# Keys of a delta-rule memory fed to the tensor engine as 32x32 blocks, without block-diagonal copies

## The reference, cut to what matters

```
S = S * exp(g)                       # decay, per head and mode
kv = k @ S                           # read the memory with the key
dv = (v - kv) * beta                 # what the memory got wrong
S = S + outer(k, dv)                 # correct it
o += mode_weight * (q @ S)           # summed over the 8 modes
```

## Time and profile before

| | us |
|---|---|
| median of 3 runs | 8003.09 |
| lowest and highest run | 7991.04 to 8010.95 |
| the profiled execution's own time | 7953.85 |
| its span, first to last instruction | 7951.7 |
| mean granted clock of the tensor engine, share of full | 0.82 |

### The profile page before, as it was taken

How to read it: one execution, slowest core, us unless ns; L and a number is a source line. 1 busy time by engine, 2 the same in 40 slices (tenths; PEclk the granted TensorE clock), 3 DMA queues, 4 the chain that set the end, 5 groups by cost and what they waited for, 6 DMA issues and landing times. The chain is left out here.

```text
span 7951.7 us, 264166 instructions
## 1 busy us (share of the span) xinstructions
PE 5413.0 (68%) x111401; PEld 4716.2 (59%) x111401; DVE 5656.2 (71%) x11457; ACT 3642.4 (46%) x7127; POOL 1241.2 (16%) x740
## 2 busy tenths in 40 slices
PE   0676667666776677666766667666676667766994
PEld 0666656556666666566665666556666556655663
DVE  6777777777777777777777787777777777776003
ACT  0454445544544455544544455544454445554220
POOL 0111111111111111111111111111111111111003
PEclk9787888777877787887878888888887888887997
DMA  2000000000000000000000000000000000000223
GB/s 75 2 6 6 6 6 4 4 6 6 6 6 6 6 4 6 4 6 6 6 6 6 6 4 6 4 6 6 6 6 6 6 6 4 6 4 9 87 75 95
DMA packets 60431, 104.35 MB, mean 13 GB/s; under 512 B 11296, under 2 KB 48736, under 8 KB 58080
## 3 DMA queue, kind: packets, MB, share of 16 engines
q1 hardware_dynamic: 50784, 61.66, 2.4%
q0 software_dynamic: 8448, 25.18, 1.0%
HBM read 53.25 MB, written 33.55 MB: 11 GB/s over the span
## 5 line engine op out<-in xcount | busy, mean ns | idle before, releaser
L765 ACT ACTIVATE state<-state,gc_end 128x128 f32<-128x128 f32 x2048 | 650.1, 389 | 1432.4 <-PE bank L569 1430.9
L563 PE MATMUL bank<-rhs,tt 32*32 32x64 f32 x16384 | 407.0, 248 | 874.7 <-DVE rhs L1256 874.6
L563 PEld LDWEIGHTS bank<-rhs,tt 32*32 32x32 f32 x16384 | 316.3, 125 | 961.5 <-issue 944.4
L582 PE MATMUL last_two<-dvs,kte 128*64 128x64 f32 x16384 | 716.4, 254 | 150.3 <-DVE dvs L1263 150.3
L634 PE MATMUL bank<-tmp,turn_mat 32*32 32x128 f32 x24576 | 745.3, 279 | 48.4 <-issue 34.1
L545 PE MATMUL bank<-state,ke 128*64 128x64 f32 x16384 | 647.3, 246 | 167.3 <-issue 128.8
L582 PEld LDWEIGHTS last_two<-dvs,kte 128*64 128x64 f32 x16384 | 655.1, 167 | 164.9 <-DVE dvs L1263 157.2
L634 PEld LDWEIGHTS bank<-tmp,turn_mat 32*32 32x32 f32 x24576 | 709.8, 110 | 71.5 <-issue 65.4
L800 ACT ACTIVATE ke<-kq 32x512 f32<-32x512 f32 x1024 | 641.9, 627 | 238.1 <-DVE kq L1191 226.0
L545 PEld LDWEIGHTS bank<-state,ke 128*64 128x64 f32 x16384 | 605.2, 159 | 238.9 <-issue 184.2
L1239 DVE TENSOR_TENSOR last_two<-last_two,prod 128x31 f32<-128x31 f32 (+15 forms) x1984 | 692.5, 349 | 68.1
(11 more groups left out here) (236 smaller groups left out, 9821.8 us busy)
## 6 DMA issues: line engine op xcount, KB each, us to landing
w_sb<-in_L_ffn_W_dram SPq DMA_DIRECT2D x16, 1024.0 KB, 9.6
expert_rows<-ke SPq DMA_DIRECT2D x1, 8192.0 KB, 21.0
xrows<-expert_rows SPq DMA_DIRECT2D x16, 512.0 KB, 8.7
expert_outputs<-yrow POOLq DMA_DIRECT2D x16, 512.0 KB, 3.4
xt<-_attn_hidden_states_dram SPq DMA_DIRECT2D x32, 128.0 KB, 2.4
xr<-_attn_hidden_states_dram SPq DMA_DIRECT2D x32, 128.0 KB, 3.0
x_after_attention<-xr SPq DMA_DIRECT2D x32, 128.0 KB, 1.7
xo<-x_after_attention SPq DMA_DIRECT2D x32, 128.0 KB, 3.6
```

The costliest lines, as they stand in the source:

```text
L563: pe.matmul(bank_mem[g][s, q % 4 * DK:q % 4 * DK + DK], tt[s, c, q, :], rhs[s, q, :], start=True, stop=True)
L582: mm = pe.matmul(bank_upd[g][s, (q % 4) * P + r * DK:(q % 4) * P + r * DK + DK], kte[:, r, q, s], dvs[:, q, :], start=True, stop=True)
L765: ins = act.activation(state[:, vh * HQ + q], state[:, vh * HQ + q], ACT.Copy, scale=gc_end[:, vh, q, c:c + 1])
```

## The change

Gram, read and update take the keys directly from `kq` and `kt`, one 32x32 matmul per mode (`MODES`, four slices of 32 partitions) in place of one 128x64 matmul per side, so each of the three groups has 128 records in place of 64. `ke`, `kte`, the ACT functions that fill them, their calls and their semaphores go. Since the copies no longer carry the keys over to the next half, `kq` and `kt` get a second buffer, chosen by `hh`. Ahead of each group of 32x32 matmuls PE gets one semaphore increment (`pe_held`), as the corrections have it already. `gram` now waits for `k_rotated`, the update for `kt_ready`. The scratch areas of the set-up move from `ke` to `kq`, and one clearing of `kte` on POOL goes.

```diff
-        kt = sb("kt", [P, 2, HQ, P])
+        kt = sb("kt", [P, 2, 2, HQ, P])
-        kq = sb("kq", [P, 2, HQ, 2, P])
-        ke = sb("ke", [P, NC, 2, HQ, P])
-        kte = sb("kte", [P, 2, HQ, P])
+        kq = sb("kq", [P, 2, 2, HQ, 2, P])
...
-            def gram(u, c):
+            def gram(u, hh, c):
...
-                pe.wait_ge(sem("ke_ready"), 4 * u + c + 1)
+                pe.wait_ge(sem("k_rotated"), since("k_rotated", u + 1))
...
+                    pe.sem_inc(sem("pe_held"), 1)
                     for q in range(HQ):
                         for r in range(2):
-                            for s in SIDES:
-                                mm = pe.matmul(b[s, q * 2 * C:(q + 1) * 2 * C], ke[:, c, r, q, s],
-                                               kq[:, r, q, :, c * C:c * C + C], start=(r == 0), stop=(r == 1))
+                            for s in MODES:
+                                mm = pe.matmul(b[s, q * 2 * C:(q + 1) * 2 * C], kq[s, hh, r, q, 0, c * C:c * C + C],
+                                               kq[s, hh, r, q, :, c * C:c * C + C], start=(r == 0), stop=(r == 1))
...
+                    pe.sem_inc(sem("pe_held"), 1)
                     for q in range(4 * g, 4 * g + 4):
                         for r in range(2):
-                            for s in SIDES:
-                                mm = pe.matmul(bank_mem[g][s, q % 4 * DK:q % 4 * DK + DK], ke[:, c, r, q, s],
-                                               state[:, hh * HQ + q, r, :], start=(r == 0), stop=(r == 1))
+                            for s in MODES:
+                                mm = pe.matmul(bank_mem[g][s, q % 4 * DK:q % 4 * DK + DK], kq[s, hh, r, q, 0, c * C:c * C + C],
+                                               state[s, hh * HQ + q, r, :], start=(r == 0), stop=(r == 1))
...
-                    pe.wait_ge(sem("kte_ready"), vc + 1)
+                    pe.wait_ge(sem("kt_ready"), v + 1)
+                    pe.sem_inc(sem("pe_held"), 1)
...
-                            for s in SIDES:
+                            for s in MODES:
                                 mm = pe.matmul(bank_upd[g][s, (q % 4) * P + r * DK:(q % 4) * P + r * DK + DK],
-                                               kte[:, r, q, s], dvs[:, q, :], start=True, stop=True)
+                                               kt[s, hh, r, q, c * C:c * C + C], dvs[s, q, :], start=True, stop=True)
...
-            def expand_kte(v, c):
...
-            def expand_ke(v, c):
...
-            def turn_keys(u, first):
-                if not first:
-                    dve.wait_ge(sem("kte_ready"), 4 * u)
-                ln(dve.transpose(kt[:, 0], kq[:, 0, :, 0, :]))
-                vec(dve.transpose(kt[:, 1], kq[:, 1, :, 0, :]), "kt_ready", u + 1)
+            def turn_keys(u, hh):
+                ln(dve.transpose(kt[:, hh, 0], kq[:, hh, 0, :, 0, :]))
+                vec(dve.transpose(kt[:, hh, 1], kq[:, hh, 1, :, 0, :]), "kt_ready", u + 1)
```

More of the change, by code:

```diff
@@ L273, in build @@
         xg = tmp[:, 3, 0:4 * P].rearrange("p (c m j) -> p c m j", c=NC, m=4)
+        scratch = kq[:].rearrange("p a r q s t -> p (a r q s t)")
         at = cos_t[:].rearrange("p q t -> p (q t)").rearrange("p (c q i) -> p c q i", c=NC, q=HQ)
@@ L279, in build @@
         sq = rhs[:].rearrange("p q v -> p (q v)").rearrange("p (h t) -> p h t", h=HH)
-        wmod_sb = ke[:].rearrange("p a b c d -> p (a b c d)")[:, 0:KC * 6 * D].rearrange("p (k n) -> p k n", k=KC)
-        onehot = ke[:].rearrange("p a b c d -> p (a b c d)")[:, 0:Q * NEXP].rearrange("p (q e) -> p q e", q=Q)
-        picked = ke[:].rearrange("p a b c d -> p (a b c d)")[:, Q * NEXP:2 * Q * NEXP].rearrange("p (q e) -> p q e", q=Q)
+        wmod_sb = scratch[:, 0:KC * 6 * D].rearrange("p (k n) -> p k n", k=KC)
+        onehot = scratch[:, 0:Q * NEXP].rearrange("p (q e) -> p q e", q=Q)
+        picked = scratch[:, Q * NEXP:2 * Q * NEXP].rearrange("p (q e) -> p q e", q=Q)
         turn_tab = qg[:].rearrange("p r q t -> p (r q t)")[:, 0:7 * NEXP].rearrange("p (k e) -> p k e", k=7)
@@ L373, in _ @@
             sp.wait_ge(sem("setup_done"), 1)
-            zero_row = ke[:].rearrange("p c r q j -> p (c r q j)")[:, 0:2048]
+            zero_row = scratch[:, 0:2048]
             sp.dma_start(slots_dram[0:E * CAP, :].rearrange("(a p g) d -> p a (g d)", p=P, g=8),
@@ L671, in half @@
                     corrections(v, vh, 3)
-                gram(u, 0)
+                gram(u, hh, 0)
                 rows(4 + hh)
                 if not first:
[L675 to L678, removed]
+                    update_and_outputs(v, vh, 3)
+                gram(u, hh, 1)
+                gram(u, hh, 2)
+                gram(u, hh, 3)
                 if hh == 0 and not first:
@@ L834, in half @@
                 for s in range(2):
-                    if s == 0 and not first:
-                        act.wait_ge(sem("upd_full1"), since("upd_full1", 4 * v + 2))
-                        expand_kte(v, 2)
                     take(lambda b: act.activation(raw[:, s].rearrange("p h t -> p (h t)"), b[:, :], ACT.Copy))
@@ L845, in half @@
                     take_dv(v, vh, 2)
-                act.wait_ge(sem("k_rotated"), since("k_rotated", u + 1))
-                expand_ke(u, 0)
-                if not first:
-                    act.wait_ge(sem("upd_full1"), since("upd_full1", 4 * v + 3))
-                    expand_kte(v, 3)
-                expand_ke(u, 1)
                 if not first:
                     take_dv(v, vh, 3)
-                expand_ke(u, 2)
-                expand_ke(u, 3)
                 clear_inverse(v, first)
@@ L881, in half @@
                     gap(n - 1)
-                if not first:
-                    act.wait_ge(sem("upd_full1"), since("upd_full1", 4 * v + 4))
-                act.wait_ge(sem("kt_ready"), u + 1)
-                expand_kte(u, 0)
             def route(t):
@@ L1052, in _ @@
             lp(dve.tensor_copy(pos[:], pos0))
-            lp(dve.memset(ke[:], 0.0))
+            lp(dve.memset(scratch, 0.0))
             lp(dve.memset(count[:], 0.0))
@@ L1190, in rotate_keys @@
                     else:
-                        vec(dve.tensor_tensor(kq[:, 1, :, 0, :], tm[0], tm[1], ALU.subtract), "k_rotated", u + 1)
+                        vec(dve.tensor_tensor(kq[:, hh, 1, :, 0, :], tm[0], tm[1], ALU.subtract), "k_rotated", u + 1)
             def beta_decays(u, hh):
@@ L1200, in beta_decays, with queries_for_memories @@
                                            dec[:, s4].rearrange("p q c i -> p (q c i)"), ALU.mult))
-            def turn_keys(u, first):
-                if not first:
-                    dve.wait_ge(sem("kte_ready"), 4 * u)
-                ln(dve.transpose(kt[:, 0], kq[:, 0, :, 0, :]))
-                vec(dve.transpose(kt[:, 1], kq[:, 1, :, 0, :]), "kt_ready", u + 1)
-            def queries_for_memories(u):
+            def turn_keys(u, hh):
+                ln(dve.transpose(kt[:, hh, 0], kq[:, hh, 0, :, 0, :]))
+                vec(dve.transpose(kt[:, hh, 1], kq[:, hh, 1, :, 0, :]), "kt_ready", u + 1)
+            def queries_for_memories(u, hh):
                 dve.wait_ge(sem("q_rotated"), since("q_rotated", u + 1))
@@ L1360, in half @@
                 memories(right_sides, 3)
-                turn_keys(u, first)
+                turn_keys(u, hh)
                 memories(decayed_corrections, 3)
                 chunk_systems(u, 0)
-                queries_for_memories(u)
+                queries_for_memories(u, hh)
                 memories(update_memories, 3)
@@ L1430, in _ @@
             pool.wait_ge(sem("setup_done"), 1)
-            vec(pool.memset(kte[:], 0.0), "clear_step", 1)
-            vec(pool.memset(ones[:], 1.0), "clear_step", 2)
+            vec(pool.memset(ones[:], 1.0), "clear_step", 1)
             for i in range(4):
```

36 lines of the change are left out of this document (16 added, 20 removed).

## The result

The changed kernel takes 8245.22 us (median of 4 runs, 8238.91 to 8247.92) against 8006.41 for the kernel before in the same comparison: ratio 1.0301, 95% interval 1.0283 to 1.0318, so 239 us slower. The forecast said slower, 8090 us, and at most 8230: the right side and the right mechanism, but a third of the size, and the result lies above its range. The profiled execution took 8247.92 us, close to the median; that of before was 0.6% quicker than its runs.

The account below looks back on a forecast made before the run. No engine full: each half is a chain between DVE, PE and ACT. Per half -0.5 + 0.6 + 1.15 = +1.25 us; 63 halves +79, with the after-loop part +88: 7953.85 becomes 8042, scaled to 8090 us; range 7950 to 8230.

Parts of the forecast that it names:

- ACT's relief: Chunk 1's second update no longer waits for ACT's key copy: 0.5 us gained a half, -31 us over 63 halves.
- Work and shape: On PE, 128 small records take 1.8 to 2.3 us against 2.09 before; shape changes add 0.4 and 0.1 us.
- The supply's price: Instruction fetching for PE: one packet, some 125 records, per 3.54 us, so 128 records take 3.6 us when starved.
- Rival 1: Instruction supply keeps up on PE, only the -31 us stand: 7972 us, range 7945 to 8003; chance 0.30.
- part (c): After the loop: 128 more records in each of three chunks, 3 us each, 9 us in all.
- Where it hits: Places of instruction shortage: chunk 1 +0.6 us a half, update 3 to last Gram +1.15, after the loop 9 in all.
- chunks up to Gram 0: Chunk 0's shape changes and chunk 1's earlier update gain 0.6 us a half; chunk 1's instruction shortage costs 0.6.
- Gram 0 itself: One change of matmul shape ahead of the first Gram product: +0.1 us a half.
- from update 3 to root or residual: 528 records in a row outrun the instruction packets: +1.5 us with `hh` 0, +0.8 with `hh` 1, mean +1.15.
- The tail of halves with `hh` 1: From update 3, the last Gram ends 13.1 us later, at 3059.6 against 3058.86 before: +0.8 us.
- Rival 2, the clock: Starved PE is granted the lower clock, a group costs 3.61 us instead of 2.09: about 8280 us; chance 0.12.

## Why the prediction was right and wrong

**ACT's relief: right.** Forecast -31 us, bounds 0 to -57; measured -22 without the added records, and PE's wait for the copy is gone.

**Work and shape: right.** 127 records took 2.00 us, 15.7 ns each, against 14.2 to 18.1 forecast; with half as many records the shape cost nothing that can be measured.

By the floor of about 25 ns in the Trainium skill, "TensorE: Matmul & The Clock Gate", section "Wait — 56ns, not 53.3ns?", 128 would have taken 3.2 us, as an estimate; the timelines contradict it.

**The supply's price: nearly right.** 125 records in 3.54 us were taken; it is 128 in 3.75. Some 1350 packets were forecast, 1342 came. Rival 1 would have had no gaps of "issue". After the loop, part (c), 9 us were forecast; from the first read there to `project_out` the two timelines differ by 10.8.

The Trainium skill, "Runtime: NRT & Kernel Launch", section "Instruction fetch mechanics", has the block of 256 instructions, and 128 pairs a packet agree; that the crossing of a block is mostly hidden, the gaps of 0.9 to 1.8 us at each block contradict.

**"Where it hits": the step that failed.** It let the shortage be felt once in the chunks, in the chain of three Grams, and nowhere else. Against the table of the result, in us a half: chunks up to Gram 0, forecast 0 net, measured 0.71; Gram 0 itself, 0.1 against 0.38; from update 3 to root or residual, 1.15 against 2.59; after that, 0 against 0.51. In sum 1.25 against 4.19, and so 8245 us came out above the range that ended at 8230. Three faults account for most of it.

- PE's stock is not full again after a stretch that it has just survived. I priced two stretches, each as though nothing were short ahead of it, the second from a packet and a half. The trace has breaks of "issue" in the reads, the update of chunk 1 and Gram 0 as well, and by Gram 1 PE has 4 records in hand in one kind of half and 55 in the other. That each place takes what is missing from the next fits this, and so does Gram at 2.5 points behind an update of 128 records against 1.25 alone; it was not measured place by place.
- Work behind a starved row starves too. The values (+1.15 us in halves with `hh` 1: +4.52 less +3.37) are long records and were costed at nothing, but they stand in the next packet. The same happens behind the residual, where in halves with `hh` 0 DVE waits for turn sums (+0.96: +3.79 less +2.83); that they are late because of PE's place in its list is read from the trace and was not tried apart.
- The tail of halves with `hh` 1 was measured against one half of rows 7, in which Gram 3 ran at the lower clock: 12.33 us from update 3 to the end of Gram 3, where the mean of 29 halves is 11.64. The mean in the changed kernel, 13.46, is close to the 13.1 forecast; the 0.8 should have been 1.5, and is 1.82.

ACT's in-order list is not a fourth. The forecast passed the lateness of Gram 3 on along it, and in the changed kernel DVE does wait 259.3 us for the root in place of 172.8; but moving the root gave both kernels the same, and the delay of PE reached DVE another way.

**Rival 2, the clock: not here.** The clock of the changed kernel is 0.828, that of before 0.820. Of the kernels of the experiments only the one with Gram doubled falls far, to 0.752; the others lie between 0.803 and 0.832.

**The range** reached to a rate of 4.3 us a packet for the counted places, not to places that were not counted.

## What to carry to other kernels

Count instructions as you count columns: here every 128 pairs of load and matmul on PE cost a packet of 3.75 us, so records shorter than about 29 ns on average (3.75 us over 128) ran dry where enough of them stood in a row, and the loss went on into what came next. Splitting a block-diagonal product into true blocks saved copies but doubled the records; it cost nothing in the update (0.9953) and 1.25 points in the dense row of Grams. That wide and slow work around the update is the reason is argued from PE's order and was not tried. And when one engine's wait is long, look for an instruction in the releaser's list whose inputs were ready much earlier: moving the root, which the change had not touched, was worth some seven times the relief of ACT's copies (0.0197 against 0.0028).

## What was not expected of the hardware

The packet of instructions holds 128 pairs (256 more packets for 32768 more records), and its price of 3.75 us is the same for records of 32 and of 64 columns, and at a granted clock of 0.50 and of 1.00. Most of that price is not the transfer: in the 14 us from 3138 of the changed kernel the queue moved 3 packets in 1.4% of the 16 engines' time, which makes about 1 us each (an estimate). What fills the rest was not found. The most starved kernel was also granted the least clock: with Gram at 256 records it is 0.752, against 0.828, and the values behind the third Gram take 5.50 us for 15 records where the changed kernel takes 3.40.
